# A transformer layer with routed experts on one core: a new order of the opening, a router product by expert, and token sums on GpSimd

## The chip, the core and the metric

The kernel runs on one core of a Trainium2 chip. The core has TensorE (matrix products into PSUM), VectorE, ScalarE and GpSimd (elementwise work; GpSimd can't read PSUM), and SyncE, which here only issues transfers. The metric is the device time of one execution in microseconds; lower is better. All four engines run instruction streams that are written out by hand and synchronise by semaphores, so an instruction that waits holds up everything behind it on its engine.

## The reference

The layer takes x of 2 x 1024 tokens by 256 features. It is normalised (`xn`), and two branches are added to x: an attention layer and a feed-forward layer, both fed with `xn`.

```python
xn = _layernorm(x, axis=-1)
x = x + _L0_attn_ref(xn, ...) + _L0_ffn_ref(xn, ...)

# attention: 16 heads of 128, causal, with a second normalisation (gain, bias) and rope
x = (h - mu) * rsqrt(var + EPS) * ln_g + ln_b
q = rope(x @ wq.T + bq); k = rope(x @ wk.T + bk); v = x @ wv.T + bv
attn = softmax(where(causal, -inf, einsum(q, k) * scale))
return einsum(attn, v) @ wo.T + bo + residual

# feed-forward: 32 experts, 4 per token from 2 of 4 groups, at most 64 tokens an expert, and a shared part
logits = x @ gate_w.T
scores = sigmoid(logits); sc = scores + gate_bias      # choice of groups, then of 4 experts
out = moe(x, topk_idx, topk_w)                          # silu(x @ w1) * (x @ w3) @ w2 per expert
shared = silu(x @ shared_gate) * (x @ shared_up) @ shared_down
return out + shared
```

## The kernel before

The tokens are four groups q of 512 (`NG`), each of four tiles of 128. Every product of 32-bit numbers is made of three: an operand is split into a high part (ScalarE rounds it, `_hi`) and a low part (the difference, `_lo`), and `three` (L296 to L298) multiplies high by high, high by low and low by high. So each operand of TensorE costs a ScalarE copy and a subtraction.

*The opening* prepares all of it, group by group. x is loaded (`xt`). `stats` (L1163, L1166, VectorE) takes mean and variance, GpSimd turns them into 1/sqrt by a power and one Newton step (`root_of`, L1604 to L1614), `norm` (L1176, VectorE) makes `xn`. A second pass over `xn` gives z (`again`, L870, ScalarE) for the attention. TensorE turns both (`turn_x` L321, `turn_z` L328), two half-width turns k per group, into features by tokens. Then come, for each q: the router's product `gate`, the shared part's `shared` (gate s=0, up s=1, two halves f) and `down`, and for unit 0 `project` (q and k), `values` and the rope. A rope (L1586, L1587, L1590, GpSimd) is three operations of 512 columns and needs a swap of halves by SyncE's transfers. The four PSUM banks of this part are handed round by the table `pro_uses`: the use number i takes bank i mod 4 and waits until use i-4 has been read.

*The loop* runs over 32 units n (a head and a batch each). In a unit TensorE makes eight score tiles, VectorE masks them and takes their maxima (`maxes`, L1439), ScalarE takes exponentials, TensorE turns the probabilities in twelve pieces (`turn`, L419; `TGROUPS`), which are split again (L1008, L1449), and multiplies them with the values (`weighted`) and the output weights (`outproj`), and VectorE adds the result to `acc` (`add_out`, L1479). These steps of neighbouring units are woven together, also with routing, expert products, and gathers and scatters of token rows in DRAM (`token_table`, `token_sum`).

*The tail* is unit 31. `weighted_part` makes its second half in two parts, each followed by `out_hi_part` (L1019), `out_lo_part` (L1467) and an output product. The experts' token sums come back as `fin_y[q]`; GpSimd adds a bias row to each (L1686), and VectorE adds them to `acc` (`add_rest`, L1507). SyncE stores the four groups as they are complete.

## Time and profile before

| | us |
|---|---|
| median of 3 runs (lowest to highest) | 1049.17 (1049.14 to 1049.52) |
| profiled execution, its own time | 1049.23 |
| its span | 1047.4 |
| TensorE busy | 1014.3 (97%) |
| VectorE busy | 727.0 (69%) |
| ScalarE busy | 659.6 (63%) |
| GpSimd busy | 754.1 (72%) |

The busy time of matmuls (PE) overlaps with that of their weight loads (PEld). The ends of matmuls are modelled, so for a stream of them the distance between starts is what one costs. The chain of work that ended last is 81% TensorE over the span. The span begins before the first transfer and ends with the last store; the time of an execution is about 1.8 us longer than the span.

### The profile page before, as it was taken

The numbers are of one execution on the slowest core, as the hardware profiler recorded it, in microseconds if no ns is written. First come the engines' busy times: TensorE is split into PE (matmuls) and PEld (weight loads), VectorE is DVE, ScalarE is ACT, GpSimd is POOL, SyncE is SP. The second block draws the span as 40 slices with busy tenths as digits, with TensorE's granted clock in tenths as the row PEclk, the third lists the DMA queues.
The fourth block names the chain that finished last, engine by engine and source line by source line (L and its number), as shares of the span: only waits on it lengthen the run. The fifth ranks groups of instructions, "written<-read, shape, count | busy, mean of one in ns | idle before, by whom it ended". The sixth has DMA issues, their size and how long they took to land.

```text
span 1047.4 us, 18814 instructions
## 1 busy us (share of the span) xinstructions
PE 1014.3 (97%) x6500; PEld 913.6 (87%) x6500; DVE 727.0 (69%) x1747; ACT 659.6 (63%) x1450; POOL 754.1 (72%) x654
## 2 busy tenths in 40 slices
PE   3999999999999999999999999999999999999997
PEld 2888888898988889899999989899998999899896
DVE  6867778877886877766666665666666666665667
ACT  4566666666666666666665566666566665666663
POOL 4735776777677775769778688877869787787770
PEclk9999999999999999999999999999999999999999
DMA  7211326212221212323332232423233332231232
GB/s 240 61 57 41 92 72 121 61 37 46 51 61 36 56 38 44 62 66 80 92 90 57 66 87 69 102 46 85 70 81 87 86 77 60 66 81 29 44 101 81
DMA packets 51629, 75.42 MB, mean 72 GB/s; under 512 B 12240, under 2 KB 29008, under 8 KB 51408
## 3 DMA queue, kind: packets, MB, share of 16 engines
q1 hardware_dynamic: 46144, 67.66, 24.3%
q0 software_dynamic: 5392, 6.56, 4.1%
q8 instruction: 53, 0.87, 0.4%
q14 instruction: 40, 0.33, 0.1%
HBM read 33.94 MB, written 10.90 MB: 43 GB/s over the span
## 4 chain that ended last, share of the span: by engine, by line
PE 81%; POOL 7%; DVE 5%; ACT 3%; DMA 2%; issue 2%; SPq 0%; DVEq 0%; POOLq 0%; ACTq 0%
PE ps L296 22%; PE ps L298 22%; PE ps L297 22%; PE ps L419 10%; PE ps L502 2%; POOL qs L1587 2%; POOL qb L1590 2%; POOL qb L1586 2%; DMA qs<-qb 2%; PE ps L514 1%; DVE ps L1439 1%; POOL q_l L1119 1%; ACT prob L997 1%; DVE acc L1479 0%; POOL root L1605 0%
## 5 line engine op out<-in xcount | busy, mean ns | idle before, releaser
L1586 POOL TENSOR_TENSOR qb<-qb,k_sb 128x512 f32<-128x512 f32 x128 | 170.5, 1332 | 208.2 <-DMA qs<-qb 207.8
L1439 DVE CUSTOM_DVE_ANT_0 ps<-ps,maskr 128x128 f32<-128x128 f32 (+7 forms) x256 | 193.8, 763 | 54.9 <-PE ps L298 54.5
L997 ACT ACTIVATE prob<-ps,nmax 128x128 f32<-128x128 f32 (+7 forms) x256 | 190.6, 744 | 60.6 <-DVE nmax L1439 58.9
L1008 ACT ACTIVATE ptd_h<-ps 128x128 fp32r<-128x128 f32 (+3 forms) x256 | 108.7, 437 | 167.5 <-PE ps L419 166.4
L1449 DVE TENSOR_TENSOR ptd_l<-ps,ptd_h 128x128 fp32r<-128x128 f32 (+3 forms) x256 | 124.7, 487 | 82.6 <-ACT ptd_h L1008 79.4
L1590 POOL TENSOR_TENSOR qb<-qb,qs 128x512 f32<-128x512 f32 x128 | 165.8, 1295 | 19.0 <-POOL qs L1587 1.0
L1587 POOL TENSOR_TENSOR qs<-qs,k_sb 128x512 f32<-128x512 f32 x128 | 175.7, 1373 | 0.0
L419 PE MATMUL ps<-k_sb,prob 128*128 128x128 f32 x1152 | 171.9, 273 | 3.0 <-DVE ptr_l L1449 1.2
L419 PEld LDWEIGHTS ps<-k_sb,prob 128*128 128x128 f32 x1152 | 135.7, 141 | 18.7 <-issue 3.0
L296 PE MATMUL ps<-k_h,q_h 128*128 128x512 f32 (+3 forms) x384 | 141.1, 368 | 3.3 <-ACT prob L997 2.9
L298 PE MATMUL ps<-k_h,q_l 128*128 128x512 f32 (+3 forms) x384 | 131.3, 342 | 0.0
L297 PE MATMUL ps<-k_l,q_h 128*128 128x512 f32 (+3 forms) x384 | 131.1, 341 | 0.0
L1479 DVE SCALAR_TENSOR_TENSOR acc<-ps,rinv,acc 128x256 f32<-128x256 f32 x256 | 111.6, 478 | 27.5 <-PE ps L298 27.3
L296 PE MATMUL ps<-x2h,wqh 128*128 128x512 f32 x256 | 108.6, 424 | 0.9 <-DVE acc L1479 0.5
L298 PE MATMUL ps<-x2h,wql 128*128 128x512 f32 x256 | 100.8, 394 | 0.0
L297 PE MATMUL ps<-x2l,wqh 128*128 128x512 f32 x256 | 100.2, 392 | 0.0
L1449 DVE TENSOR_TENSOR ptr_l<-ps,ptr_h 128x512 fp32r<-128x512 f32 x128 | 88.0, 688 | 9.2 <-ACT ptr_h L1008 6.3
L1008 ACT ACTIVATE ptr_h<-ps 128x512 fp32r<-128x512 f32 x128 | 76.0, 594 | 15.9 <-PE ps L419 15.0
L296 PEld LDWEIGHTS ps<-k_h,q_h 128*128 128x128 f32 x384 | 72.5, 189 | 15.0 <-ACT prob L997 7.2
L296 PE MATMUL ps<-ptd_h,v_h 128*128 128x256 f32 (+3 forms) x258 | 84.8, 329 | 0.0
L298 PE MATMUL ps<-ptd_h,v_l 128*128 128x256 f32 (+3 forms) x258 | 83.0, 322 | 0.0
L1119 POOL TENSOR_TENSOR q_l<-qb,q_h 128x512 fp32r<-128x512 f32 x62 | 81.1, 1308 | 2.0 <-ACT q_h L808 1.5
(178 smaller groups left out, 2611.9 us busy)
## 6 DMA issues: line engine op xcount, KB each, us to landing
qs<-qb SPq DMA_DIRECT2D x256, 128.0 KB
ew<-epack SPq DMA_DIRECT2D x16, 768.0 KB, 4.3
rqk<-wqk SPq DMA_DIRECT2D x16, 256.0 KB, 2.9
xt<-x SPq DMA_DIRECT2D x4, 512.0 KB, 4.7
rv<-wvp SPq DMA_DIRECT2D x8, 256.0 KB, 3.3
ro<-wop SPq DMA_DIRECT2D x16, 128.0 KB, 2.3
token_table<-xn SPq DMA_DIRECT2D x4, 512.0 KB, 4.6
token_sum<-token_table SPq DMA_DIRECT2D x1, 2048.0 KB, 9.9
```

The lines of the kernel that those rows point to most:

```text
L296: eng.matmul(dst, lhs[0], rhs[0], start=start, stop=False)
L297: eng.matmul(dst, lhs[0], rhs[1], start=False, stop=False)
L298: return eng.matmul(dst, lhs[1], rhs[0], start=False, stop=stop)
L419: ins = pe.transpose(bank[:, j * P:(j + 1) * P], prob[:, t % 2, (j0 + j) * P:(j0 + j + 1) * P], ident)
L997: act.activation(prob[:, t % 2, 0:w], tile[t], ACT.Exp, bias=nmax[:, t:t + 1], scale=-1.0, accum_out=rsum[:, t:t + 1]).then_inc(exp_done, 1)
L1008: act.activation(turned(0, t, j0, w), src, ACT.Copy).then_inc(pth_done, 1)
L1439: dve.tensor_tensor_reduce(out=tile[t], in0=tile[t], in1=maskr[:, SEQ - w:SEQ], scale=-1.0, scalar=3e38, op0=ALU.add, op1=ALU.min, accum_o ...
L1449: dve.tensor_tensor(turned(1, t, j0, w), src, turned(0, t, j0, w).bitcast(F32), ALU.subtract).then_inc(ptl_done, 1)
L1479: ins = dve.scalar_tensor_tensor(out=acc[:, t, :], in0=rbank("OP", u, c, i2)[:, i * DM:(i + 1) * DM], scalar=rinv[:, j:j + 1], in1=acc[:, ...
L1586: pool.tensor_tensor(qb[:, i, :], qb[:, i, :], cos_sb[:, c], ALU.mult).then_inc(rope_a, 1)
L1587: pool.tensor_tensor(qs[:, i % 2, :], qs[:, i % 2, :], sin_sb[:, c], ALU.mult).then_inc(rope_b, 1)
L1590: pool.tensor_tensor(qb[:, i, :], qb[:, i, :], qs[:, i % 2, :], ALU.add).then_inc(rope_t, 1)
```

## The change

*The opening.* The first 512 KB of x are loaded in halves, one issued by SyncE and one by ScalarE; the shared part's first two weights are issued before the second group of x, and each of the three has a semaphore of its own. For the first group, the root's last steps move from GpSimd to VectorE (`first_root`: three steps, and for z a fourth), and TensorE turns each tile as it is normalised (`turn_tiles`). The order of all further steps is another one on every engine, and so is the table of banks. GpSimd makes seven lo parts that were VectorE's: the value weights', the third shared weight's, head 1's projection weights' and the four of z in groups 2 and 3.

*The router.* High and low parts of its weight stand side by side in one operand of 64 columns, `gws`. The product comes out as experts by tokens, two products of 512 columns for each of two k; ScalarE copies it (`lgt`), TensorE turns it back in four pieces (`gate_turn`), and VectorE adds the high and low halves (`logits`). So a fourth product, low by low, is now among them.

*The tail.* GpSimd makes the four additions of `add_rest`, and VectorE's are gone. TensorE makes turns 8 to 11 first, then a weighted part, an output product of two halves, the second weighted part, and the last output product.

```diff
+            def turn_tiles(src, name, tile_ready, last_ready):
+                banks = [popen(name, 0, k) for k in range(KC)]
+                for i in range(GT):
+                    pe.wait_ge(*((tile_ready, i + 1) if i < GT - 1 else (last_ready, 1)))
+                    for k in range(KC):
+                        ins = pe.transpose(banks[k][:, i * P:(i + 1) * P], src[:, 0, i, k * P:(k + 1) * P], ident)
...
             def gate(q):
...
-                for i in range(GT):
-                    for k in range(KC):
-                        ins = three(pe, bank[:, i * EXPERTS:(i + 1) * EXPERTS],
-                                    (xnh[q % 2][:, k, i * P:(i + 1) * P], xnl[q % 2][:, k, i * P:(i + 1) * P]),
-                                    (gwh[:, k, :], gwl[:, k, :]), k == 0, k == KC - 1)
+                for k in range(KC):
+                    pe.matmul(bank, gws[:, k, :], xnh[q % 2][:, k, :], start=(k == 0), stop=False)
+                    ins = pe.matmul(bank, gws[:, k, :], xnl[q % 2][:, k, :], start=False, stop=(k == KC - 1))
+                ins.then_inc(pro_done, 1)
+
+            def gate_turn(q):
+                pe.wait_ge(*freed("gate", q))
+                bank = popen("gt", q)
                 for i in range(GT):
+                    ins = pe.transpose(bank[:, 2 * i * EXPERTS:2 * (i + 1) * EXPERTS], lgt[:, i * P:(i + 1) * P],
+                                       ident[0:2 * EXPERTS, 0:2 * EXPERTS])
...
             pe.wait_ge(id_in, 16)
-            turn_x(0, 0)
-            turn_x(0, 1)
-            turn_z(0, 0)
-            turn_z(0, 1)
-            turn_x(1, 0)
+            turn_tiles(xn, "xt", xn_tile, xn_ready)
+            turn_tiles(zz, "zt", z_tile, z_ready)
+            gate(0)
             shared(0, 0, 0)
...
             u = UNITS - 1
             turn(u, 8)
             turn(u, 9)
+            turn(u, 10)
+            turn(u, 11)
+            weighted_part(u, 0)
             outproj(u, 0, 0)
             outproj(u, 0, 1)
-            weighted_part(u, 0)
-            turn(u, 10)
-            turn(u, 11)
+            weighted_part(u, 1)
             outproj(u, 1, 0)
-            weighted_part(u, 1)
             outproj(u, 1, 1)
...
-            sp.dma_start(xt[:, 0, :, :], x_t[0]).then_inc(x_in[0], 16)
+            sp.dma_start(xt[:, 0, 0:2, :], x_t[0][:, 0:2, :]).then_inc(x_in[0], 16)
             sp.dma_start(k_sb[:, 0:2 * P], cst[:, 0:2 * P]).then_inc(id_in, 16)
+            sp.dma_start(shw[0], sh_gate).then_inc(sw_in[0], 16)
+            sp.dma_start(shw[1], sh_up).then_inc(sw_in[1], 16)
             sp.dma_start(xt[:, 1, :, :], x_t[1]).then_inc(x_in[1], 16)
...
+            act.dma_start(xt[:, 0, 2:4, :], x_t[0][:, 2:4, :]).then_inc(x_half, 16)
...
+            def first_root(s):
+                dve.wait_ge(pow_ready, s + 1)
+                stepped(dve.tensor_tensor(newton[:, s, :], root[:, s, :], root[:, s, :], ALU.mult))
+                stepped(dve.scalar_tensor_tensor(out=newton[:, s, :], in0=newton[:, s, :], scalar=-0.5, in1=var[:, s, :],
+                                                 op0=ALU.mult, op1=ALU.mult))
+                stepped(dve.scalar_tensor_tensor(out=rstd[:, s, :], in0=newton[:, s, :], scalar=1.5, in1=root[:, s, :],
+                                                 op0=ALU.add, op1=ALU.mult))
+                if s:
+                    dve.scalar_tensor_tensor(out=shift[:, 0, :], in0=mv[:, 1, :, 0], scalar=-1.0, in1=rstd[:, 1, :],
+                                             op0=ALU.mult, op1=ALU.mult).then_inc(first_ready, 1)
...
+            def logits(q):
+                dve.wait_ge(pro_done, pcount("gt", q))
+                bank = pbank("gt", q)[:, 0:2 * GT * EXPERTS].rearrange("p (i s e) -> p i e s", s=2, e=EXPERTS)
+                dve.tensor_reduce(sg[:, q * GT:(q + 1) * GT, :], bank, AX.X, ALU.add).then_inc(pfree("gt", q), 1)
...
-            add_rest(u, 2)
+            turned_lo(u, 10)
+            turned_lo(u, 11)
+            recips(u, 1)
             dve.wait_ge(yadd_done, 3)
             add_out(u, 0, 0)
+            out_lo_part(u, 0)
             add_out(u, 0, 1)
-            out_lo_part(u, 0)
-            turned_lo(u, 10)
-            turned_lo(u, 11)
-            add_rest(u, 3)
-            recips(u, 1)
+            out_lo_part(u, 1)
             dve.wait_ge(yadd_done, 4)
...
             root_of(0, 0, 1)
-            root_of(1, 0, 2)
-            root_of(0, 1, 3)
+            root_of(0, 1, 2)
+            root_of(1, 0, 3)
+            wv_lo(pool, 0)
+            pool.wait_ge(swl_ready, 2)
+            shared_lo_w(pool, 2)
             root_of(1, 1, 4)
...
-            root_of(2, 1, 7)
+            root_of(3, 0, 7)
+            pool.wait_ge(wql_done, 1)
+            wqk_lo(pool, 1)
+            pool.wait_ge(x2l_ready, 2 * KC)
+            z_lo(pool, 2, 0)
             root_of(3, 1, 8)
+            z_lo(pool, 2, 1)
+            z_lo(pool, 3, 0)
+            z_lo(pool, 3, 1)
...
+            for q in range(NG):
+                pool.wait_ge(yc_done, q + 1)
+                pool.wait_ge(add_done, 4 * (UNITS - 1 if q >= NG // 2 else UNITS - 2))
+                dst = acc[:, GT * q:GT * (q + 1), :]
+                pool.tensor_tensor(dst, fin_y[q][:, :, :], dst, ALU.add).then_inc(yadd_done, 1)
```

Three places show how the instructions stand. VectorE, from the first statistics on, before:

```order
L1163 BN_STATS st<-xt 128x6 x4
L1166 BN_AGGR mv<-st 128x2 x4
L1163 BN_STATS st<-xt 128x6 x4
L1166 BN_AGGR mv<-st 128x2 x4
L1176 TENSOR_SCALAR xn<-xt,mv,rstd 128x256 x4
L1163 BN_STATS st<-xn 128x6 x4
L1166 BN_AGGR mv<-st 128x2 x4
L1131 TENSOR_TENSOR wql<-rqk,wqh 128x512
L1196 TENSOR_TENSOR swl<-ra_,swh 128x512
```

and now:

```order
L1204 BN_STATS st<-xt 128x6 x4
L1207 BN_AGGR mv<-st 128x2 x4
L1166 TENSOR_TENSOR swl<-ra_,swh 128x512
L1213 TENSOR_TENSOR newton<-root 128x4
L1214 SCALAR_TENSOR_TENSOR newton<-newton,var 128x4
L1216 SCALAR_TENSOR_TENSOR rstd<-newton,root 128x4
L1230 TENSOR_SCALAR xn<-xt,mv,rstd 128x256 x4
L1204 BN_STATS st<-xn 128x6 x4
L1207 BN_AGGR mv<-st 128x2 x4
L1204 BN_STATS st<-xt 128x6 x4
L1207 BN_AGGR mv<-st 128x2 x4
L1213 TENSOR_TENSOR newton<-root 128x4
```

The second group's statistics moved behind the first group's normalisation and second statistics; a weight's lo part and three steps of the root came in front of it, and the second root's steps (the last row is the first of four) stand behind the second group's statistics.

TensorE at the first group's router product, before (the three rows of `gwh` and `gwl` come eight times):

```order
L298 MATMUL ps<-x2h,wql 128x512
L296 MATMUL ps<-gwh,xnh 128x32
L297 MATMUL ps<-gwl,xnh 128x32
L298 MATMUL ps<-gwh,xnl 128x32
...
L328 MATMUL ps<-k_sb,zz 128x128 x8
```

and now (the two rows of `gws` come twice):

```order
L335 MATMUL ps<-k_sb,xn 128x128 x8
L335 MATMUL ps<-k_sb,zz 128x128 x8
L352 MATMUL ps<-xnh,gws 64x512
L353 MATMUL ps<-xnl,gws 64x512
...
L301 MATMUL ps<-xnh,swh 128x512
```

It stood behind the first two projections and stands now directly behind the turns of z.

VectorE at the end of unit 31, from the largest maximum on, before:

```order
L1439 ISA ps,nmax<-ps,maskr 128x1024
L1439 ISA nmax 128x1
L1449 TENSOR_TENSOR ptr_l<-ps,ptr_h 128x4x128
L1449 TENSOR_TENSOR ptd_l<-ps,ptd_h 128x2x128
L1507 TENSOR_TENSOR acc<-fin_y,acc 128x1024
L1462 TENSOR_TENSOR ol<-ps,oh 128x512
L1449 TENSOR_TENSOR ptr_l<-ps,ptr_h 128x4x128
L1449 TENSOR_TENSOR ptd_l<-ps,ptd_h 128x3x128
L1507 TENSOR_TENSOR acc<-fin_y,acc 128x1024
L1479 SCALAR_TENSOR_TENSOR acc<-ps,rinv,acc 128x256 x4
L1467 TENSOR_TENSOR ol<-ps,oh 128x256
```

and now:

```order
L1491 ISA ps,nmax<-ps,maskr 128x1024
L1491 ISA nmax 128x1
L1501 TENSOR_TENSOR ptr_l<-ps,ptr_h 128x4x128
L1501 TENSOR_TENSOR ptd_l<-ps,ptd_h 128x2x128
L1514 TENSOR_TENSOR ol<-ps,oh 128x512
L1501 TENSOR_TENSOR ptr_l<-ps,ptr_h 128x4x128
L1501 TENSOR_TENSOR ptd_l<-ps,ptd_h 128x3x128
L1501 TENSOR_TENSOR ptr_l<-ps,ptr_h 128x4x128
L1501 TENSOR_TENSOR ptd_l<-ps,ptd_h 128x4x128
L1508 RECIPROCAL rinv<-rsum 128x4
L1531 SCALAR_TENSOR_TENSOR acc<-ps,rinv,acc 128x256 x2
L1519 TENSOR_TENSOR ol<-ps,oh 128x256
```

The additions of `fin_y` are gone from between the lo parts, and all four lo parts of the last turns stand ahead of the first addition to `acc`.

## Rows read from the trace of the kernel before

**Rows 1.** Busy time by stretch: us, then each engine's, granted clock, DMA share, GB/s.

```profile
0.00:21.00 21.00, 3.90 (x17) 3.53 (x18) 13.49 (x47) 7.45 (x13) 10.37 (x31) 1.00 0.88 299
21.00:87.20 66.20, 64.25 (x415) 57.39 (x414) 48.50 (x95) 42.15 (x80) 34.08 (x46) 1.00 0.19 51
87.20:1031.60 944.40, 936.43 (x5998) 843.78 (x5997) 655.04 (x1587) 607.10 (x1351) 709.65 (x578) 1.00 0.28 68
```

**Rows 2.** What TensorE waited for, 21 to 87.2 us: total, times, longest.

```profile
PE ps L296 <- DVE sth L1210: 1.1, 1, 1.1
PE ps L328 <- ACT acc L907: 0.7, 1, 0.7
```

**Rows 3.** Timeline, 0 to 35 us: start, duration, instruction, idle time before it.

```profile
4.73 1.41 DVE L1163 BATCH_NORM_STATS2 st<-xt 128x6 f32<-128x256 f32 x4 [3.03 <-DMA xt<-x]
...
7.06 1.05 POOL L1605 TENSOR_TENSOR root<-var,power 128x4 f32<-128x4 f32 x1
...
9.28 1.39 DVE L1176 TENSOR_SCALAR xn<-xt,mv,rstd 128x256 f32<-128x256 f32 x4 [0.87 <-POOL rstd L1610]
...
12.61 0.58 POOL L1604 TENSOR_SCALAR var<-mv 128x4 f32<-128x4 f32 x1 [0.57 <-DVE mv L1166]
...
13.27 1.44 POOL L1605 TENSOR_TENSOR root<-var,power 128x4 f32<-128x4 f32 x1
...
16.91 2.08 ACT L870 ACTIVATE zz<-xn,shift,rstd 128x256 f32<-128x256 f32 x4 [2.56 <-POOL shift L1614]
...
19.04 1.97 PE L328 MATMUL ps<-k_sb,zz 128*128 128x128 f32 x8 [6.29 <-ACT zz L870]
```

**Rows 4.** Timeline of TensorE in two places, matmuls of 512 columns.

```profile
22.95 0.63 PE L296 MATMUL ps<-xnh,swh 128*128 128x512 f32 x1
...
23.37 0.63 PE L297 MATMUL ps<-xnl,swh 128*128 128x512 f32 x1
...
25.25 0.40 PE L296 MATMUL ps<-xnh,swh 128*128 128x512 f32 x1
...
25.49 0.39 PE L297 MATMUL ps<-xnl,swh 128*128 128x512 f32 x1
```

**Rows 5.** Timeline of TensorE: first and last of the router's 24 matmuls.

```profile
30.04 0.18 PE L296 MATMUL ps<-gwh,xnh 128*128 128x32 f32 x1
...
32.53 0.26 PE L298 MATMUL ps<-gwh,xnl 128*128 128x32 f32 x1
```

**Rows 6.** Costliest groups: busy us, mean ns of one, idle before.

```profile
L1587 POOL TENSOR_TENSOR qs<-qs,k_sb 128x512 f32<-128x512 f32 x128 | 175.7, 1373 | 0.0
```

**Rows 7.** Timeline of VectorE: lo parts of z, alone and beside a rope.

```profile
21.67 0.69 DVE L1188 TENSOR_TENSOR x2l<-ztmp,x2h 128x512 fp32r<-128x512 f32 x1 [3.16 <-ACT x2h L885]
...
35.50 3.28 DVE L1188 TENSOR_TENSOR x2l<-ztmp,x2h 128x512 fp32r<-128x512 f32 x2 [1.24 <-ACT x2h L885]
```

**Rows 8.** Timeline of TensorE in the tail.

```profile
1032.68 0.39 PE L296 MATMUL ps<-woh,oh 128*128 128x256 f32 x1 [1.02 <-DVE ol L1462]
...
1034.22 0.28 PE L296 MATMUL ps<-ptr_h,v_h 128*128 128x256 f32 x1
...
1036.30 1.06 PE L419 MATMUL ps<-k_sb,prob 128*128 128x128 f32 x8
...
1038.93 0.39 PE L296 MATMUL ps<-ptr_h,v_h 128*128 128x256 f32 x1 [0.56 <-DVE ptd_l L1449]
...
1042.93 0.39 PE L296 MATMUL ps<-woh,oh 128*128 128x256 f32 x1 [0.93 <-DVE ol L1467]
```

**Rows 9.** Timeline of VectorE in the tail.

```profile
1030.80 1.22 DVE L1507 TENSOR_TENSOR acc<-fin_y,acc 128x1024 f32<-128x1024 f32 x1
...
1031.94 0.69 DVE L1462 TENSOR_TENSOR ol<-ps,oh 128x512 fp32r<-128x512 f32 x1
...
1043.94 0.88 DVE L1479 SCALAR_TENSOR_TENSOR acc<-ps,rinv,acc 128x256 f32<-128x256 f32 x2 [1.07 <-PE ps L298]
```

**Rows 10.** Timeline of GpSimd's last instructions.

```profile
1011.63 9.46 POOL L1686 TENSOR_TENSOR fin_y<-fin_y,cbc 128x1024 f32<-128x1024 f32 x4
```

More of the change, by code:

```diff
@@ L579, in _ @@
             down(2, 1)
-            shared(3, 0, 1)
+            turn_z(3, 0)
             shared(3, 1, 1)
-            turn_z(3, 0)
             turn_z(3, 1)
-            gate(3)
-            values(0, 3)
+            project(1, 0)
+            gate_turn(3)
             down(3, 0)
@@ L871, in again @@
                                          scale=rstd[:, 2 * q + 1, i:i + 1])
+                    if q == 0 and i < GT - 1:
+                        ins.then_inc(z_tile, 1)
                 ins.then_inc(z_ready, 1)
@@ L888, in logits @@
                 bank = drop("gate", q)
-                act.activation(sg[:, q * GT:(q + 1) * GT, :].rearrange("p a b -> p (a b)"), bank[:, 0:GT * EXPERTS],
-                               ACT.Copy).then_inc(pfree("gate", q), 1)
+                if q:
+                    act.wait_ge(pro_done, pcount("gt", q - 1))
+                act.activation(lgt[:, :], bank[0:2 * EXPERTS, :], ACT.Copy).then_inc(pfree("gate", q), 1)
             def shared_tanh(q, f):
@@ L1177, in norm @@
                                             rstd[:, 2 * q, i:i + 1], ALU.subtract, ALU.mult)
+                    if q == 0 and i < GT - 1:
+                        ins.then_inc(xn_tile, 1)
                 ins.then_inc(xn_ready, 1)
@@ L1604, in root_of @@
                 stepped(pool.tensor_scalar(var[:, j, :], mv[:, j, :, 1], EPS, None, ALU.add))
+                if q == 0:
+                    pool.tensor_tensor(root[:, j, :], var[:, j, :], power[:, :], ALU.pow).then_inc(pow_ready, 1)
+                    return
                 stepped(pool.tensor_tensor(root[:, j, :], var[:, j, :], power[:, :], ALU.pow))
```

283 lines of the change are left out of this document (144 added, 139 removed), and 13 rows, old and new, of the table pro_uses.

## The prediction

> **What bounds the kernel now.** I read the busy times by stretch first, then what TensorE waits for in the opening, then the first 21 us and the last 17 us in order of time. The stretches [rows 1]: in the first 21.0 us TensorE is busy 3.9 us. From 21.0 to 87.2, where the shared feed-forward part and unit 0 are prepared, it is busy 64.25 of 66.2 us. From 87.2 to 1031.6, the loop over 32 units, it is busy 936.4 of 944.4. So TensorE sets the pace from 21 us on, while in the opening VectorE is busy 48.5 of 66.2 us, ScalarE 42.2 and GpSimd 34.1. TensorE's waits there are small, 1.1 and 0.7 us [rows 2]. Work taken from it there and an earlier start both shorten the kernel, as long as the others keep up. The loop is edited only in its last unit; each unit waits for things of its own and of the unit before, so I take a shift at the loop's start to arrive whole at its end.
>
> The first 21 us are one chain [rows 3]: x lands and its statistics start at 4.73, GpSimd's power starts at 7.06 and takes 1.05, the normalisation starts on VectorE at 9.28 and takes 1.39, GpSimd takes up the second root at 12.61, its power takes 1.44, ScalarE makes z from 16.91 in 2.08, and TensorE turns z from 19.04 in 1.97, so it comes to its long work at 21.01.
>
> **The opening's chain.** The half load: four tiles of statistics take 1.41 [rows 3], so at most the 0.7 us of two tiles goes under the second half. It can also give nothing, since both halves share the DMA engines with the other first transfers. I take 0.4. The shorter root: between the power's end, 8.11, and the normalisation's start lie 1.17 us of four GpSimd steps, 0.29 each. Three VectorE steps stand there now. The trace has none like them; 0.29 is one bound and 0.1 the other (four aggregations, a GpSimd step and the hand-over fit into the 0.92 between the statistics and the power). I take 0.25, so 0.75 for the three: 0.4 gained. VectorE's lo part of a weight, ahead of them, should pass while GpSimd takes the power. Normalisation then starts at 8.45, 0.8 earlier, and GpSimd takes up the second root 0.9 earlier, at 11.7, since no other root stands ahead. Its step and power should take 1.4, to 13.1; they took 2.1 where the first root's took 1.4. VectorE is then in the second group's statistics (1.41 and some 0.4, from 11.65) until 13.45, and four steps of 0.25 end at 14.45, where ScalarE began at 16.91: 2.4 gained. Last, three tiles of z are turned while the later ones are made, and the fourth's two turns cost 0.5 (eight took 1.97). TensorE begins its long work at 14.45 + 2.08 + 0.5 = 17.05, against 21.01: **3.9 us gained**. From both sides: 2.4 if the turns by tile give nothing, 4.8 with the full half load and steps of 0.1.
>
> **The slow stretch.** Matmuls of 512 columns start 0.42 us apart at 22.95 and 0.24 apart at 25.25 [rows 4]: TensorE's lower clock level (1.2 GHz) and its higher one (2.4), though the stretches' granted clock reads 1.00 [rows 1]. It had waited 6.3 us before 19.04, and was slow for some 5 us after. So from 21.01 on the slow part cost about 1.6 us over the fast price. Now each tile of z gives 0.5 us of turns while the next takes 0.52, from 15.0 on, nearly a full stream, so the slow part should end near 20.2 and cost 1.6 again: no term.
> The Trainium skill ("TensorE: Matmul & The Clock Gate", Part 1: The HAM clock gate) says that the array runs at half clock until it has been active. By that rule the gaps between the turns could count against it, and the sum would be about 1 us worse; no row here tells it.
>
> **The router product.** Before, a group's product is 24 matmuls of 32 columns from 30.04 to 32.64 [rows 5], 0.11 each. Now it is 4 matmuls of 512 columns at 0.24 [rows 4], 0.95 us, and later four turns. Eight turns took 1.06 [rows 8], so four take 0.53. The saving is 2.60 - 1.48 = 1.12 a group, for 4 groups **4.5 us** (5.4 if the half-height turns cost half, 3.5 if each of the eight new pieces pays 0.12 to start). ScalarE's copy of the product becomes 512 long instead of 128 and VectorE gets four short sums; both have room [rows 1].
>
> **Waits.** The 1.8 us [rows 2] belong to the old order; I count them as gone and walk the new one. GpSimd gets seven lo parts of 512 columns. A piece with two inputs takes it 1.37 [rows 6], so 9.6 us on top of 34.1, in some 62. In its queue stand the ropes of three such pieces (4.1 us), each behind its swap: I find the four ropes at 29.7, 33.5, 41 and 46, the last root ending near 60 and TensorE asking for the last z near 70. The added work is hidden by some 7 us of slack. I find TensorE waiting at the third projection, for the lo part of group 1's z (1 us), at the second group's up product, for the router's short sum to free a bank (0.5), and at the last down products (0.5). I add 1 us for the two engines' contention: VectorE's lo part of z took 0.69 alone at 21.67 and 3.28 for two at 35.50, with GpSimd in a rope [rows 7]. **3.0 us of new waits** (0 if all fits, 6 if the contention does what the first rival says).
> The Trainium skill ("SBUF — State Buffer", SBUF: two separate sides) says that a VectorE instruction with two SBUF inputs and GpSimd's take a shared port pair as a lock, each for a whole instruction. The 3.28 agrees. By that rule each of the seven pieces can hold VectorE up once.
>
> **The tail.** Before [rows 8], TensorE waits 1.02, makes an output product (1032.68 to 1034.22), a weighted part to 1036.30, eight turns to 1037.39, half an output product, waits 0.56, the second weighted part from 1038.93 to about 1042.0, waits 0.93 and makes the last half. VectorE's last addition starts at 1043.94 and takes 0.88 [rows 9]; the span ends 2.6 later, after the last store. Now the turns stand first. Four of the eight fill the wait of 1.02. The other four need the bank that the lo part at 1031.94 frees; the addition of 1.22 at 1030.80 [rows 9] goes from ahead of it to GpSimd, and it moves up by 0.8, so the turns end at 1032.4. The first weighted part starts there and not at 1034.22: 1.8 gained. From its start to the last product's end the old order takes 9.7 us, 1.5 of them waits. The new one puts a half product between the second weighted part and the half that waits for its lo part: the turns' 1.06 is gone and the output product's 1.54 comes in, 0.4 of the waits stay, and it takes some 8.4. Together **3.1 us gained** (1.0 if the first weighted part starts hardly earlier, 3.5 with no wait left). GpSimd pays four additions of 1024 columns. Its four of that shape took 9.46 from 1011.63 [rows 10], 2.37 each. Two follow to 1025.9 and two, behind unit 30's last addition near 1028, to 1033; VectorE asks for the third near 1035 and the fourth near 1040. The cover breaks only if one takes over 3.5 us.
>
> **Sum**, against the profiled execution, with a span of 1047.40 and a time of 1049.23 (the median shown is 1049.17, so nothing is corrected): 1049.2 - 3.9 - 4.5 - 1.8 + 3.0 - 3.1 = **1038.9 us**.
>
> **Rivals.**
> *The opening starves.* Each of GpSimd's seven added pieces costs its 1.37 where TensorE waits, 9.6 us, less some 3.5 that slack hides: 6 us of new waits and not 3. For it: the 3.28 [rows 7], and that GpSimd works strictly in its written order. Against: VectorE loses seven pieces. 1041.9, chance 0.14.
> *The early start is lost.* The halves land together, VectorE's weight piece falls under the power and delays both, and the slow clock lasts: 3.9 becomes 1.5. For it: the second root's power of 1.44 against 1.05 [rows 3]. This is the case in which the change does in part not do what it says. 1041.3, chance 0.12.
> *No new waits.* Then 3.0 is nought. Against: the old order had 1.8. 1035.9, chance 0.13.
> *The tail waits for GpSimd.* Its additions run slower than the four before them and hold VectorE's last ones, and 3.1 is lost. Against: they have the same shape. 1042.0, chance 0.04.
> *Slower.* GpSimd's queue becomes the opening's bound: at the rate that the pieces show beside VectorE the last root moves from 60 past 67, where the slack ends, and each us beyond it is a us of TensorE. It decides once that root ends some 12 us later still, near 79, for which its queue from 17 us on would have to stretch by half. With 1.5 us more, 1050.5, chance 0.03.
> My forecast has the rest, 0.54.
>
> **Range and chances.** The range goes from no waits with the tail at its best, 1035.5, to the starved opening with a part of the start lost, 1043.3. A difference under 0.2% (2.1 us) can't be told from none; only mild forms of the slower case lie there. Faster 0.95, within 0.01, slower 0.04.
>
> **What would show it.** The router's first matmul at 17.0 (right between 16.5 and 18); unit 0's first scores near 80 against 87.3; a router product of about 0.95 us; TensorE's busy time less by 4 to 5 us; no wait of VectorE for GpSimd in the tail. Wrong would be: a wait of TensorE above 1.5 us between 17 and 80 us that a root or a rope ends (the first rival), z begun after 16 (the second), or a loop that is longer than the 944.4 us before, by which the shift would not arrive.

## The result, and the profile after

| | before | after |
|---|---|---|
| median, us (lowest to highest, runs) | 1049.31 (1049.14 to 1049.52, 4) | 1042.78 (1041.59 to 1044.33, 4) |
| ratio, 95% interval | | 0.9939 (0.9921 to 0.9956) |
| profiled execution, span | 1049.23, 1047.4 | 1042.93, 1040.8 |
| unit 0's first scores | 87.26 | 77.65 |
| unit 31's first scores | 1006.44 | 1002.47 |
| loop: unit 0's first scores to unit 31's | 919.18 | 924.82 |
| tail: from there to the span's end | 40.96 | 38.33 |
| TensorE busy | 1014.3 | 1010.5 |

Faster, and inside the range of 1035.5 to 1043.3, but 3.9 us over the forecast of 1038.9. The three stretches of the profile say where (a unit begins with its first score product on TensorE): the opening gave 9.6 us and not 7.2, the tail 2.6 and not 3.1, and the loop, whose code is the same, took 5.6 us more.

The opening after, in order of time (start, duration, instruction, idle before it); it answers to [rows 3].

```profile
4.27 1.40 DVE L1204 BATCH_NORM_STATS2 st<-xt 128x6 f32<-128x256 f32 x4 [2.58 <-DMA xt<-x]
...
6.61 1.31 POOL L1647 TENSOR_TENSOR root<-var,power 128x4 f32<-128x4 f32 x1
7.95 0.16 DVE L1213 TENSOR_TENSOR newton<-root 128x4 f32<-128x4 f32 x1 [0.95 <-POOL root L1647]
8.15 0.16 DVE L1214 SCALAR_TENSOR_TENSOR newton<-newton,var 128x4 f32<-128x4 f32 x1
8.35 0.16 DVE L1216 SCALAR_TENSOR_TENSOR rstd<-newton,root 128x4 f32<-128x4 f32 x1
8.55 1.38 DVE L1230 TENSOR_SCALAR xn<-xt,mv,rstd 128x256 f32<-128x256 f32 x4
...
14.16 2.08 ACT L897 ACTIVATE zz<-xn,shift,rstd 128x256 f32<-128x256 f32 x4 [1.03 <-DVE shift L1219]
...
14.82 2.17 PE L335 MATMUL ps<-k_sb,zz 128*128 128x128 f32 x8 [3.77 <-ACT zz L897]
...
16.16 2.31 DVE L1230 TENSOR_SCALAR xn<-xt,mv,rstd 128x256 f32<-128x256 f32 x4
16.63 0.78 PE L352 MATMUL ps<-xnh,gws 128*64 128x512 f32 x1
...
18.06 0.63 PE L353 MATMUL ps<-xnl,gws 128*64 128x512 f32 x1
...
18.49 0.49 PE L301 MATMUL ps<-xnh,swh 128*128 128x512 f32 x1
...
18.81 0.39 PE L302 MATMUL ps<-xnl,swh 128*128 128x512 f32 x1
```

The reader sees VectorE's three steps 0.20 apart, z begun at 14.16, and the router's product standing first on TensorE at 16.63. Its matmuls start 0.43 apart, the lower clock level, and from 18.81 on 0.23 apart, the higher: TensorE was slow for 2.1 us of its long work (from 16.63 to 18.7), and before for 3.2 (from 20.8 to 24.0) [rows 4]. What TensorE waits for from there to unit 0 is 2.0 us (waited for: total, times, longest), against [rows 2]:

```profile
PE ps L301 <- DVE sth L1257: 1.4, 1, 1.4
PE ps L326 <- DVE xnl L1238: 0.6, 1, 0.6
```

A router product of a later group with the turns of the group before it, to [rows 5]: four matmuls in 1.00 us, four turns in 0.40.

```profile
30.00 0.39 PE L352 MATMUL ps<-xnh,gws 128*64 128x512 f32 x1
...
30.68 0.40 PE L353 MATMUL ps<-xnl,gws 128*64 128x512 f32 x1
31.00 0.46 PE L360 MATMUL ps<-k_sb,lgt 64*128 64x64 f32 x4
31.40 0.66 PE L326 MATMUL ps<-k_sb,xn 128*128 128x128 f32 x4
```

**Where the loop loses.** The loop's 5.6 us build up mostly in steps of 0.8 to 1.4 in units 2, 6, 8, 10, 12 and 14 (6.3 by unit 15). Behind them units 20 and 26 are 0.8 and 1.1 longer than before, and units 18 and 24 are 1.5 and 1.0 shorter. Unit 6 on TensorE, after (first three lines) and before (the last):

```profile
239.19 0.30 PE L301 MATMUL ps<-k_h,q_h 128*128 128x128 f32 x1 [0.16 <-POOL q_l L1149]
...
241.67 0.63 PE L440 MATMUL ps<-k_sb,prob 128*128 128x128 f32 x4 [0.25 <-DVE ol L1514]
...
244.50 0.44 PE L301 MATMUL ps<-k_h,q_h 128*128 128x384 f32 x1 [0.66 <-ACT prob L1028]
```

```profile
252.31 0.44 PE L296 MATMUL ps<-k_h,q_h 128*128 128x384 f32 x1 [0.49 <-ACT prob L997]
```

The waits name GpSimd, VectorE and ScalarE, and they make 0.6 of the 0.8 us that this unit is longer. What is late behind them is the rope of this unit's q and k, which GpSimd makes in the unit before. Before, in unit 5 (it begins at 219.55), the swap's third piece is issued 18.73 us into the unit and GpSimd's rope starts 2.90 later:

```profile
238.28 0.46 SPq L689 DMA_DIRECT2D qs<-qb  x1
...
239.63 0.46 SPq L689 DMA_DIRECT2D qs<-qb  x1
```

```profile
241.18 1.30 POOL L1586 TENSOR_TENSOR qb<-qb,k_sb 128x512 f32<-128x512 f32 x1 [5.54 <-DMA qs<-qb]
```

After, unit 5 begins at 210.62. The issue is again 18.72 into the unit, but the rope starts 4.21 after it, and the fourth piece's issue (230.69) takes 1.57 instead of 0.46:

```profile
229.34 0.46 SPq L712 DMA_DIRECT2D qs<-qb  x1
229.84 0.60 SPq L713 DMA_DIRECT2D qs<-qb  x1
230.69 1.57 SPq L712 DMA_DIRECT2D qs<-qb  x1
```

```profile
233.55 1.28 POOL L1627 TENSOR_TENSOR qb<-qb,k_sb 128x512 f32<-128x512 f32 x1 [6.87 <-DMA qs<-qb]
```

What lies there is one packet of another DMA queue. First the whole program's line of the page (packets, MB, share of 16 engines), then the swap's queue (q1) and the same one in the 0.25 us from 230.50:

```profile
q8 instruction: 53, 0.87, 0.4%
...
q1 hardware_dynamic: 23, 0.05, 85.2%
q8 instruction: 1, 0.02, 34.3%
```

34.3% of 16 engines over 0.25 us is 1.37 us of one engine. So this instruction fetch of 16 KB holds one of the sixteen DMA engines for 1.37 us, from 230.51 to 231.89. The swap's packets (q1) fill 85.2% of the sixteen in the same 0.25 us, so it is spread over nearly all of them, and it lands 1.3 us late. The trace shows what is late. From 231.86 to 232.90 only eight more packets of the queue q1 start, one behind the other (the same view for that stretch):

```profile
q1 hardware_dynamic: 8, 0.01, 6.7%
```

6.7% of 16 engines is the time of one engine: the swap's last packets run singly there, from the fetch's end on, while the other fifteen stand idle. The same sits in units 7, 9, 11 and 13 after (19.7 to 20.0 us into the unit), and in units 19 and 25 (20.8 and 20.9), while before, the fetch in units 5 to 13 stands at 10.5 to 12.7. The 53 fetches go with TensorE's instructions (6500 products and 6500 weight loads before, some 245 to a fetch; before_pad64, with 128 more, has 54). The router's product took 128 of them out ahead of the loop, about half an interval.

The kernel before pays for the same thing, only elsewhere. Its units 18 and 24 take 32.6 and 32.1 us and their neighbours 31.1. In units 17 and 23, ahead of them, a fetch stands at 21.7 and 20.7, and the rope starts 1.6 and 1.1 us late. In the even units there is slack: in unit 14 of the kernel before a fetch at 18.1 makes the rope 1.3 late, and no unit is longer for it.

### The profile page after: what moved, and what is told of

Read it like the earlier page. It is cut to its first block, busy times and chain, and to the rows that moved or that the text cites. A ratio compares the mean times of both kernels' runs of the same rounds, so it can differ in the third digit from the quotient of the medians.

```text
span 1040.8 us, 18702 instructions
## 1 busy us (share of the span) xinstructions
PE 1010.5 (97%) x6436; PEld 904.9 (87%) x6436; DVE 721.9 (69%) x1747; ACT 658.0 (63%) x1450; POOL 768.1 (74%) x655
## 4 chain that ended last, share of the span: by engine, by line
PE 76%; POOL 10%; DVE 5%; ACT 4%; DMA 3%; issue 2%; SPq 0%; DVEq 0%; POOLq 0%; ACTq 0%
PE ps L301 21%; PE ps L303 21%; PE ps L302 21%; PE ps L440 9%; DMA qs<-qb 3%; POOL qb L1631 3%; POOL qb L1627 3%; POOL qs L1628 3%; PE ps L523 2%; POOL q_l L1149 1%; PE ps L535 1%; ACT prob L1028 1%; DVE ps L1491 1%; ACT qb L823 1%; ACT ptr_h L1039 1%
## 5 line engine op out<-in xcount | busy, mean ns | idle before, releaser
L1631 POOL TENSOR_TENSOR qb<-qb,qs 128x512 f32<-128x512 f32 x128 | 166.7, 1302 | 18.7 <-POOL qs L1628 0.4
L301 PEld LDWEIGHTS ps<-k_h,q_h 128*128 128x128 f32 x384 | 72.5, 189 | 18.1 <-ACT prob L1028 9.9
L302 PE MATMUL ps<-ptd_l,v_h 128*128 128x256 f32 (+3 forms) x258 | 82.5, 320 | 0.0
```

The source lines that it names most:

```text
L301: eng.matmul(dst, lhs[0], rhs[0], start=start, stop=False)
L302: eng.matmul(dst, lhs[0], rhs[1], start=False, stop=False)
L1631: pool.tensor_tensor(qb[:, i, :], qb[:, i, :], qs[:, i % 2, :], ALU.add).then_inc(rope_t, 1)
```

## The experiments

TensorE's instructions ahead of the loop are counted against the kernel before. Times in us; unit 0, loop, tail and span are those of the profiled execution. The median of the kernel before was 1048.9 to 1049.3 each time that it ran beside the others.

| kernel | instructions | unit 0 | loop | tail | span | median |
|---|---|---|---|---|---|---|
| before | 0 | 87.26 | 919.18 | 40.96 | 1047.4 | 1049.3 |
| before_tail | 0 | 87.64 | 918.50 | 38.36 | 1044.5 | 1046.77 |
| after_oldgate | 0 | 86.07 | 918.46 | 38.37 | 1042.9 | 1045.68 |
| after_pad64 | 0 | 78.72 | 919.13 | 38.35 | 1036.2 | 1038.44 |
| before_router_pad64 | 0 | 98.22 | 919.47 | 40.91 | 1058.6 | 1059.50 |
| before_late | 0 | 87.14 | 923.16 | 40.90 | 1051.2 | 1053.07 |
| after_pad32 | -64 | 78.02 | 917.01 | 38.37 | 1033.4 | 1036.24 |
| after | -128 | 77.65 | 924.82 | 38.33 | 1040.8 | 1042.78 |
| after_wholex | -128 | 78.57 | 924.73 | 38.40 | 1041.7 | 1043.80 |
| after_poolroot | -128 | 81.02 | 922.92 | 38.36 | 1042.3 | 1044.70 |
| after_allturns | -128 | 80.15 | 925.27 | 38.38 | 1043.8 | 1045.58 |
| after_swapact | -128 | 78.39 | 927.32 | 38.39 | 1044.1 | 1046.16 |
| before_router | -128 | 97.58 | 925.31 | 40.91 | 1063.8 | 1064.76 |
| before_pad64 | +128 | 87.71 | 925.37 | 40.92 | 1054.0 | 1056.76 |

**The instructions put back, and put in front of the old kernel.** The edit, in both kernels around the first group's turns (in the kernel before around `turn_x(0, 0)` and `turn_x(0, 1)`):

```diff
+            def pad(k):
+                for _ in range(k):
+                    pe.transpose(ps[:, 3, 0:32], ident[0:32, :], ident[0:32, 0:32])
             pe.wait_ge(id_in, 16)
+            pad(36)
             turn_tiles(xn, "xt", xn_tile, xn_ready)
+            pad(28)
             turn_tiles(zz, "zt", z_tile, z_ready)
```

after_pad64:

> The changed kernel with 64 small TensorE turns (32 columns each, their product is used by nobody) put into its idle time in the opening, 36 ahead of the first group's turns and 28 behind them. That puts back the 128 TensorE instructions (64 products, 64 weight loads) which the router's new product took out ahead of the loop. Measured so far: loop (first scores of unit 0 to first scores of unit 31) 919.2 before and 924.8 after, time 1042.8 after. Theory A (the phase of TensorE's instruction fetches against SyncE's swap issues): the long swap issues of units 5, 7, 9, 11 and 13 go back to 0.46 us, the loop to 919 to 920.5, the time to 1037 (1036 to 1038.5). Theory B (GpSimd's rope chain limits the loop, so a head start of TensorE is lost whatever is fetched when): loop 924 to 925.5, time 1042.8. Both: unit 0's first scores at 77.6, up to 1 us earlier if the small turns raise the clock sooner.

Measured 1038.44 (1038.24 to 1038.67), ratio to before 0.9895 (0.9880 to 0.9910). Loop 919.13, as before the change. Unit 0 starts 1.1 later and not earlier: x landed 0.34 later in that run, and the clock rose at 20.1 instead of 18.8. The small turns did not bring it up. Units 18 and 24 are 0.8 and 1.4 us longer than those of the changed kernel, as a fetch stands at 20.8 and 20.7 in the units ahead of them.

before_pad64:

> The kernel before with the same 64 small turns in its opening's idle time (their product is used by nobody): 128 TensorE instructions more ahead of the loop, where the changed kernel has 128 fewer. Half a fetch interval either way, so the same phase as the changed kernel's. Theory A: the swap issues of units 5 to 13 become long, the loop grows from 919.2 to 923 to 926, the time to 1053 to 1056, with unit 0 starting where it did (87.3). Theory B: nothing moves, 1049.2 (1048 to 1049.6), loop 919 to 920.

Measured 1056.76, ratio 1.0071 (1.0057 to 1.0084); loop 925.37, with like steps in units 2 to 14. One is missing, and it fits: in unit 9 the fetch stands at 18.8 and not at 20, and unit 10 is only 0.2 longer. The kernel before has no earlier start here, so theory B falls: no head start is needed to lose 6 us. The whole moved by 7.4, a little more than theory A had.

after_pad32 (16 and 16 turns, which is 64 instructions):

> The changed kernel with 32 small turns in the opening (unused product), 64 instructions: a quarter of a fetch interval, not a half. By theory A the fetches stand some 4.6 us earlier in each unit than in the changed kernel, at about 15 us into the odd units 5 to 13, where SyncE issues nothing; the even units' fetch comes near 6.2, beside another piece of the swap (6.8). So the losses of units 5 to 13 go, and some may come elsewhere: loop 919 to 922, time 1037.5 to 1040. If only the full count of before helps (something else than the phase), or theory B: 1042.8, loop 924 to 925.

Measured 1036.24 (1035.51 to 1038.51), ratio 0.9884 (0.9868 to 0.9899): the fastest version. It beats both kernels: the changed one's interval was 0.9921 to 0.9956. Its loop is 917.0, which is 2.2 less than before: units 18 and 24 take 31.1 too, since the fetch stands at 22.4 and 22.3 in the units ahead of them and no rope is late. In units 5 to 13 the odd units' fetch stands at 12.7 to 13.4, not at 15, and every swap issue is quick; unit 5 begins at 210.46:

```profile
229.18 0.46 SPq L718 DMA_DIRECT2D qs<-qb  x1
...
230.54 0.46 SPq L718 DMA_DIRECT2D qs<-qb  x1
```

```profile
232.13 1.29 POOL L1633 TENSOR_TENSOR qb<-qb,k_sb 128x512 f32<-128x512 f32 x1 [5.57 <-DMA qs<-qb]
```

**The late swap without a fetch.**

```diff
+        def late(sp, m, i):
+            if i == 2 and m in (6, 8, 10, 12, 14):
+                for _ in range(2):
+                    sp.dma_start(spare[:, 2 * nsp[0]:2 * nsp[0] + 2], cst[:, 0:2]).then_inc(spared, 16)
+                    nsp[0] += 1
...
         def swap(sp, m, i):
...
+            late(sp, m, i)
             half = DK // 2
```

> The kernel before with two more DMA issues (8 bytes a partition, into a tile that nobody reads) on SyncE ahead of the swap's third piece for units 6, 8, 10, 12 and 14: two issues of about 0.46 us each hold the swap up by 0.9 to 1.0 us in units 5, 7, 9, 11 and 13, at the same place (20.07 us into the unit) at which the changed kernel's issues took 1.26 to 1.71. TensorE's instructions and their fetches stay as they are. If a late swap issue is what costs TensorE its time, units 6 to 14 lose 0.6 to 0.9 each, up to five times: loop 919.2 + 3 to 5 = 922 to 924, time 1052 to 1054. If the long issues are only a sign of something else (the fetch itself holding TensorE up), the chain's slack hides 1 us: loop 919 to 920, time 1049.3.

Measured 1053.07 (1052.16 to 1054.42), ratio 1.0039 (1.0025 to 1.0052); loop 923.16. One thing in my expectation was wrong: the long issue was the fourth piece's, 20.07 into the unit, while this edit holds up the third, 18.7 into it. That is the better test, because the rope that was late is the third piece's. In unit 5 (from 219.63) the rope starts at 242.09, which is 22.46 into the unit against 21.63 in the kernel before, and 0.7 to 1.0 us are lost in each of units 6, 8, 10, 12 and 14:

```profile
238.35 0.81 SPq L687 DMA_DIRECT2D spare<-cst  x2
239.20 0.47 SPq L700 DMA_DIRECT2D qs<-qb  x1
```

```profile
242.09 1.29 POOL L1597 TENSOR_TENSOR qb<-qb,k_sb 128x512 f32<-128x512 f32 x1 [6.39 <-DMA qs<-qb]
```

So 0.8 us of a late swap in five units, with TensorE's instructions where they were, costs 4.0 us of the loop: the chain from swap to rope to scores has no slack in these odd units.

**Another engine issues the swap.**

```diff
+            if not (i == 2 and m in (6, 8, 10, 12, 14)):
                 sp.dma_start(qs[0:half, i % 2, :], qb[half:DK, i, :]).then_inc(swapped[i % 2], 16)
...
+                if i == 2 and m in (6, 8, 10, 12, 14):
+                    act.wait_ge(qb_done, 4 * m + i + 1)
+                    act.wait_ge(rope_t, 4 * m + i - 1)
+                    act.dma_start(qs[0:DK // 2, 0, :], qb[DK // 2:DK, 2, :]).then_inc(swapped[0], 16)
```

> The changed kernel with five of its DMA issues moved: the first half of the swap's third piece for units 6, 8, 10, 12 and 14 (the ones whose issue took 1.26 to 1.71 us) is issued by ScalarE right behind its own copy, not by SyncE. TensorE's instructions and fetches stay. If a fetch holds up only SyncE's issues: the five losses go, loop 920.5 to 922, time 1038.5 to 1040. If it holds up whichever engine issues at that moment: ScalarE's issue becomes long and its own work behind it late, loop 924 to 926, time 1042 to 1044.

Measured 1046.16 (1043.34 to 1048.27), ratio 0.9967 (0.9949 to 0.9984), loop 927.32: nothing was won back, though whether it is worse than the changed kernel (0.9921 to 0.9956) is not clear of noise. Neither line of the expectation has it right. This edit too moved the third piece, and no issue was long in unit 5 (from 213.47), yet the rope is late as ever, 23.13 into the unit:

```profile
232.19 0.52 ACTq L828 DMA_DIRECT2D qs<-qb  x1
```

```profile
236.60 1.29 POOL L1632 TENSOR_TENSOR qb<-qb,k_sb 128x512 f32<-128x512 f32 x1 [7.04 <-DMA qs<-qb]
```

In unit 9, where this kernel's fetch stands at 18.7 and not near 20, the rope is on time, 21.6 into the unit. So the loss hangs on the landing, not on the issuing engine, and the long issue is a second sign of the held DMA engine. Of the further 2.5 us of the loop, 2.1 are lost in units 1 to 4, ahead of the first issue that was moved; they are not the price of the edit, and what made them was not settled.

**The router's product undone in the changed kernel.** `gate` makes the 24 products of 32 columns again, ScalarE copies them to `sg`, `gate_turn` and VectorE's `logits` go.

```diff
-                for k in range(KC):
-                    pe.matmul(bank, gws[:, k, :], xnh[q % 2][:, k, :], start=(k == 0), stop=False)
-                    ins = pe.matmul(bank, gws[:, k, :], xnl[q % 2][:, k, :], start=False, stop=(k == KC - 1))
+                for i in range(GT):
+                    for k in range(KC):
+                        ins = three(pe, bank[:, i * EXPERTS:(i + 1) * EXPERTS],
...
```

> The changed kernel with the router's product of before: 24 products of 32 columns a group, no turns of it, no short sums. Its own saving is lost: 4 groups of 1.12 us by my prediction, and more if the new one was better than I put it. Unit 0's first scores at 82 (77.65 + 4.5). It also has the instruction count of before. Theory A: the loop goes back to 919 to 920.5, so the time is 1042.8 + 4.5 - 5.4 = about 1042 (1041 to 1043). Theory B, if the start of TensorE's head start alone decides: the loop is somewhere between, 922 to 925, and the time 1044 to 1047.

Measured 1045.68 (1045.04 to 1047.10), 3.7 over theory A's 1042. The loop went back to 918.46, as theory A said, but unit 0 starts at 86.07, 8.4 us later and not 4.5. The first group's product is now the first long work, and TensorE is at its lower level there (0.21 apart):

```profile
17.11 0.38 PE L300 MATMUL ps<-gwh,xnh 128*128 128x32 f32 x1
17.32 0.37 PE L301 MATMUL ps<-gwl,xnh 128*128 128x32 f32 x1
...
22.23 0.77 PE L300 MATMUL ps<-xnh,swh 128*128 128x512 f32 x1
...
27.48 0.39 PE L300 MATMUL ps<-xnh,swh 128*128 128x512 f32 x1
```

It takes 5.1 us where the new one takes 1.9, and the higher level comes at 27.5, after twelve more products of 512 columns (5.25 us, against 2.8 at 0.23 each), where the changed kernel had it from its fifth on. In this order, and in this one profiled execution, the new product is worth nearly twice its price at the higher level.

**The new product alone in the kernel before.** The reverse of that edit, with `gate_turn` and `logits` put in at places of my choosing: gt 0 behind xt (2, 1), gt 1 behind g (2, 0), gt 2 behind zt (2, 1), gt 3 behind gate 3 in the table of banks.

```diff
-            ... ("gate", 1), ("xt", 2, 1), ("u", 1, 0), ...
+            ... ("gate", 1), ("xt", 2, 1), ("gt", 0), ("u", 1, 0), ...
```

> The kernel before with the router's new product alone (four products of 512 columns a group, four turns, the short sum on VectorE); opening order, start and tail as before. It takes 128 TensorE instructions out ahead of the loop. By my prediction's term it saves 4 x 1.12 = 4.5 us of the opening: unit 0's first scores at 82.8 (82.2 to 84) against 87.3. Theory A (phase of the instruction fetches): the loop then grows by the 5.6 to 6.2 us that two kernels have shown at this phase, and the time is 1049.3 - 4.5 + 5.9 = 1050.7 (1049.8 to 1052): the saving is not to be seen, or the kernel is slower. Theory B (the loop keeps what it is given): 1044.8, loop 919.

> The run before_router with the 64 small turns (their product is used by nobody) in the opening's idle time, which put the 128 instructions back. Theory A: loop back to 918.5 to 920, time 1044.8 to 1045.8, the router's saving whole. Theory B: as before_router, whatever that is, within 1 us.

Measured 1064.76 and 1059.50. The two differ by 5.3 us, and their loops by 5.8 (925.31 and 919.47), as theory A said. But unit 0 starts at 97.6 and 98.2, 15 us later than I expected: four more users of four banks in an order that was made without them. TensorE's clock fell to its lower level twice besides, at the end of the two longest of these waits, for 3.4 us each time. Among TensorE's waits (before_router):

```profile
PE ps L346 <- ACT acc L919: 3.9, 1, 3.9
PE ps L297 <- DVE sg L1218: 2.5, 1, 2.5
PE ps L297 <- ACT lgt L902: 1.5, 1, 1.5
```

What the product saves by itself in the old order is thus not measured; it needs an order of its own.

**The tail alone in the kernel before.**

```diff
             u = UNITS - 1
             turn(u, 8)
             turn(u, 9)
+            turn(u, 10)
+            turn(u, 11)
+            weighted_part(u, 0)
             outproj(u, 0, 0)
             outproj(u, 0, 1)
-            weighted_part(u, 0)
-            turn(u, 10)
-            turn(u, 11)
+            weighted_part(u, 1)
             outproj(u, 1, 0)
-            weighted_part(u, 1)
             outproj(u, 1, 1)
...
```

> The kernel before with the change's tail alone (the last unit's turns first, half products in the new order, the last token sums by GpSimd). The traces put the tail from unit 31's first scores to the end at 40.96 before and 38.33 after. If the tail's gain is its own: 1049.2 - 2.6 = 1046.6 (1046 to 1047.2). My prediction had 3.1: 1046.1. Rival: a part of the 2.63 comes from the opening's shift (what is behind at unit 31), then 1047.5 to 1048.5. Loop unchanged in all cases, 919 to 920.

Measured 1046.77 (1046.25 to 1048.22, 11 runs), ratio 0.9981 (0.9971 to 0.9990). The tail is 38.36 here and 38.33 to 38.40 in all nine kernels that have it, whenever their unit 31 starts: its 2.6 us are its own.

**Three parts of the opening undone, one at a time.**

The half load:

```diff
-            sp.dma_start(xt[:, 0, 0:2, :], x_t[0][:, 0:2, :]).then_inc(x_in[0], 16)
+            sp.dma_start(xt[:, 0, :, :], x_t[0]).then_inc(x_in[0], 16)
...
-            act.dma_start(xt[:, 0, 2:4, :], x_t[0][:, 2:4, :]).then_inc(x_half, 16)
```

> The changed kernel with its first load whole on SyncE's queue again. My prediction's term for the half load is 0.4 us (0 to 0.7): statistics begin at 4.7 instead of 4.27, z's turns at 15.2 instead of 14.82, unit 0's first scores at 78.05 (77.65 to 78.35). If the halves gain more by sharing the DMA engines better: 78.5 or later. The same instructions on TensorE, so the loop at 924 to 926.

Unit 0 at 78.57: 0.9 later. Statistics begin at 4.71 (0.44 later), z's turns at 15.24 (0.42), and the higher clock level comes at 20.2 and not at 18.8, which makes the rest. Over all kernels the statistics begin at 4.71 to 5.22 with the whole load (seven) and at 4.27 to 4.61 with the halves (seven); the means differ by 0.46.

The root's last steps, on GpSimd again (VectorE's three go):

```diff
-                    pool.tensor_tensor(root[:, j, :], var[:, j, :], power[:, :], ALU.pow).then_inc(pow_ready, 1)
+                    stepped(pool.tensor_tensor(root[:, j, :], var[:, j, :], power[:, :], ALU.pow))
+                    ...
+                    pool.tensor_tensor(rstd[:, j, :], root[:, j, :], newton[:, j, :], ALU.mult).then_inc(pow_ready, 1)
```

> The changed kernel with the first group's two roots finished by GpSimd in four steps (0.29 us each in the profile before) where VectorE now takes three of 0.20. Each root is later by 1.17 - 0.60 = 0.57: the normalisation at 9.1, z's turns at 15.9 to 16.0, unit 0's first scores at 78.8. If VectorE's own work ahead of the second root hides a part: 78.2. My prediction's own term was 0.4 for the first root. Loop 924 to 926.

z's turns start at 15.80, 0.98 later, as expected (1.1). Unit 0 is 3.4 later, though: the higher level comes at 21.6 (0.9 more), and TensorE falls back to the lower one from 55.7 to 59.1 (1.4 more), 1.3 us behind the end of a wait of 1.4 that the changed kernel has too, there without a fall:

```profile
55.42 0.28 PE L303 MATMUL ps<-swh,shl 128*128 128x256 f32 x1
...
58.20 0.41 PE L302 MATMUL ps<-wvl,x2h 128*128 128x256 f32 x1
58.41 0.41 PE L303 MATMUL ps<-wvh,x2l 128*128 128x256 f32 x1
```

The granted clock tells the same, and it shows such falls in four more of the fourteen kernels: before_late and before_tail (twice each), before_router (twice) and before_router_pad64 (twice). Stretches with each engine's busy time, granted clock, DMA share and GB/s, the first of after_poolroot and the second of before_late:

```profile
55.70:59.00 3.30, 3.30 (x17) 3.15 (x16) 3.27 (x10) 1.11 (x2) 2.42 (x2) 0.50 0.09 28
...
32.80:36.20 3.40, 3.40 (x12) 2.72 (x11) 2.13 (x7) 3.33 (x7) 3.26 (x4) 0.50 0.30 67
```

In before_late TensorE had just made the 24 products of 32 columns of a group (29.39 to 31.99). The kernel before makes the same ones from 30.04 on, and its clock did not fall. So a single execution's start of unit 0 carries a term of the clock that the edits here do not set.

The turns by tile:

```diff
-                    pe.wait_ge(*((tile_ready, i + 1) if i < GT - 1 else (last_ready, 1)))
+                    pe.wait_ge(last_ready, 1)
```

> The changed kernel with TensorE's turns of the first group waiting for the last tile of xn and of z, not for each. My prediction's term for the turns by tile is 1.5 us at z (1.97 of turns, of which 0.5 stay behind the last tile), and the same at xn, which is hidden if the chain runs through the statistics of xn and not through its turns: router's first matmul at 18.1, unit 0's first scores at 79.1. If the slow clock also lasts longer, by up to 1 us more: 80. Loop 924 to 926.

The router's first matmul at 18.49, 1.86 later, of which 0.32 is x landing later in this run: the turns by tile are worth 1.5, as put. Unit 0 at 80.15, 2.5 later; a longer slow part (0.3) and a wait longer by 0.3 are in it.

## Why the prediction was right and wrong

**The step that failed** is the first part's last sentence: "so I take a shift at the loop's start to arrive whole at its end". 5.6 us of it did not. The reason that the argument gives (each unit waits for its own things and those of the unit before) held: the loop is insensitive to when it starts, by 919.13 in after_pad64 (start 8.5 us earlier) and 918.46 in after_oldgate. It is sensitive to how many TensorE instructions stand ahead of it, for which the prediction had no term. The count moves the instruction fetches, and these decide which swap is in flight when one of the sixteen DMA engines is held for 1.37 us. The page had the queue in its list, 53 packets and 0.4% of the DMA time, and I passed over it. My own sign for being wrong, "a loop that is longer than the 944.4 us before", is what was seen. With the loop of before the forecast would have been 1.7 too high, not 3.9 too low. That the time is inside the range all the same is luck: the range's upper end was made of a starved opening and a lost start, and neither came.

**The opening's chain**, 3.9 forecast, 4.2 measured: what follows z's turns starts at 16.63, and before at 20.81. (The prediction's 21.01 is the modelled end of the turns, not the start of the work behind them; against it the gain would read 4.4.) The half load gave 0.46 (0.4 put). The root's steps took 0.20 each (0.25 put); from the power's end to the normalisation 0.63 us instead of 1.17. Against that the power took 1.31 beside VectorE's lo part, where I let it pass free. The second root went as worked out: VectorE's steps end at 14.13 (14.45 put), and the turns by tile leave 0.5 behind the last tile of z.

**The slow stretch**, no term: the higher level came 2.1 us after the start of the long work, before after 3.2. That is some 0.5 us gained here, but over the kernels of the table (without after_oldgate) the stretch from the start of the long work to the higher level varies from 1.7 to 3.9 us. It is not the opening's order that sets it: before, before_late and before_tail have the same one and show 3.2, 1.7 and 1.7. At 0.43 against 0.23 a product, that is up to 1.0 us between two executions, and the sum has no term for it. The rule of the Trainium skill ("TensorE: Matmul & The Clock Gate", Part 1: The HAM clock gate), weighed in the prediction, would have made it 1 us worse; it was not.

**The router product**, 4.5 forecast: a group takes 1.40 (1.00 and 0.40) against 2.60, so 4.8. The turns of half height cost 0.10 each, less than the 0.13 that I took. after_oldgate shows 8.4 in this order, because the first group's product now stands where TensorE is slow.

**Waits**, 1.8 gone and 3.0 new forecast: 2.0 new. The largest, 1.4, stands at the second group's down product, where I had put nothing before the last ones (0.5). The product has its low part `shl` at 51.78; what it waits for is its bank, which VectorE frees with its step on the third group's gate (`sth`), done at 52.38:

```profile
47.63 1.78 DVE L1268 TENSOR_TENSOR shl<-sth,shh 128x512 fp32r<-128x512 f32 x1
...
51.10 0.68 DVE L1268 TENSOR_TENSOR shl<-sth,shh 128x512 fp32r<-128x512 f32 x1
51.71 0.67 DVE L1257 SCALAR_TENSOR_TENSOR sth<-sth,ps 128x512 f32<-128x512 f32 x1
```

The first rival, with GpSimd's added pieces starving TensorE, did not come. The contention is there. A lo part with two SBUF inputs took 1.78 at 47.63, beside a rope's piece on GpSimd from 47.12 to 48.86; this agrees with the rule of the Trainium skill ("SBUF — State Buffer", SBUF: two separate sides) that the prediction gives. The same step at 51.10 took 0.68 and was not held by a root's power on GpSimd from 51.02 to 52.08. The stretched one stands ahead of the largest wait, so part of the 1.4 may be its doing; no run here tells how much. A normalisation of 1.38, with one tensor input, took 2.31 at 16.16 beside a lo part on GpSimd from 16.08, and TensorE waited for nothing until 39.80. Together -4.2 - 4.8 - 1.8 + 2.0 - 0.5 = -9.3; the measured shift is 9.6, and 0.3 stays open.

**The tail**, 3.1 forecast, 2.6 measured. The first weighted part starts 26.4 us into unit 31 and not 27.8: 1.4 gained (1.8 put). From there to the last product's end it takes 8.5 instead of 9.7 (8.4 put). The 8.4 does not follow from the prediction's own terms, which give 9.7 - 1.5 - 1.06 + 1.54 + 0.4 = 9.1 and a tail gain of 2.4; that it came so near is luck. TensorE still waits 0.51 for the lo part that frees the turns' bank, and 0.18 at the end:

```profile
1028.26 0.63 PE L440 MATMUL ps<-k_sb,prob 128*128 128x128 f32 x4 [0.51 <-DVE ol L1514]
...
1036.37 0.38 PE L301 MATMUL ps<-woh,oh 128*128 128x256 f32 x1 [0.18 <-DVE ol L1519]
```

GpSimd's additions take 2.4 each, and VectorE never waits for them, as forecast.

## What to carry to other kernels

Before costing a change in one stage, look where it shifts what is fixed by instruction count: removing or adding TensorE instructions in one place can move 16 KB instruction fetches against latency-bound transfers hundreds of us later, here for 5.6 us, more than any term of the sum. When a change gains less (or more) than its own stage shows, compare the start of every loop step in both traces and look for transfers that land late; then add a few idle-time instructions and measure again before judging the change. Here 32 small turns that compute nothing are worth some 6 us (0.9884 against 0.9939 of the kernel before). And a comparison of two builds needs this care on both sides: the kernel before was losing 2.5 us in the same way.

## What was not expected of the hardware

- One instruction fetch of 16 KB held one DMA engine for 1.37 us (0.88 to 1.71 over the 53 of the changed kernel). A transfer of 128 KB in flight landed 1.3 us late, whichever engine had issued it, and the DMA issue behind it on SyncE took 1.26 to 1.71 us instead of 0.46.
- TensorE at its lower level made 24 products of 32 columns in 5.1 us and was still there behind them (after_oldgate); with 64 small turns before the long work the higher level came no sooner (20.1 against 18.8).
- The time from the start of the long work to the higher level differs by up to 2.3 us (1.66 to 3.92, without after_oldgate), and by 1.5 between kernels with the same opening. In the openings of five of the fourteen kernels the clock fell back, nine times in all, for 3.4 us each time but one (6.8 in before_router_pad64). Four of the nine came 0.7 to 0.8 us behind a group's 24 products of 32 columns (before_late and before_tail), where the kernel before did the same work without a fall. What sets the rises and the falls is open.
- What makes the fetches fall where they do within a unit (64 instructions more moved them by 7.0 us in unit 5, but by 1.8 in unit 6) is open too; no run here tells.
